# Cross-attention keys prepared inside the query head, first score row begun in its last steps, 3 MB of weights loaded at its end

## The reference

```
x = x + xattn(layernorm(x), ctx)
x = x + attn(layernorm(x))          # 16 heads of 32, with rotation
x = x + ffn(layernorm(x))           # 1408 hidden, ternary weights, int8-like activations
xattn(h, c), 16 heads of 128:
  q     = h @ Wq.T                       # per head 256 x 128
  q_big = rope(q @ w_kc_q[head])         # 256 x 384
  q_r   = q_big @ W_qr[head]             # 256 x 64
  kv_r  = rope(c)                        # 4096 x 128, shared by the heads
  k_r   = kv_r @ W_kr[head]
  attn  = softmax(q_r @ k_r.T)           # 256 x 4096
  ctx   = (attn @ kv_r) @ w_kc_kv[head].T
  out   = concat(ctx) @ Wo.T
```

## Time and profile before

| | |
|---|---|
| median of 3 runs | 612.31 us (609.09 to 613.04) |
| the profiled execution's own time | 611.09 us |
| its span, mean granted TensorE clock | 609.0 us, 0.975 |
| TensorE busy | 543.2 us (89%) |
| DVE busy | 501.3 us (82%) |
| ACT busy | 378.8 us (62%) |
| POOL busy | 169.1 us (28%) |
| DMA moved | 107.40 MB |

### The profile page before, as it was taken

One profiled execution on the slowest core, in us unless ns is written; L12 is line 12 of the kernel. 1 busy time (PEld: TensorE's weight loads), 2 busy tenths in 40 slices (PEclk: granted clock), 3 DMA queues, 4 the chain that ended last, 5 costly groups with the idle time before them and its releaser, 6 DMA issues.

```text
span 609.0 us, 9985 instructions
## 1 busy us (share of the span) xinstructions
PE 543.2 (89%) x3759; PEld 359.7 (59%) x3762; DVE 501.3 (82%) x769; ACT 378.8 (62%) x487; POOL 169.1 (28%) x146
## 2 busy tenths in 40 slices
PE   6989938799989989999999999999979997788896
PEld 3767613266666657666666666666767853355543
DVE  4698858998988888898899998999966656799786
ACT  3154445877767776876767868778785348553332
POOL 0599853001222212212212120210000243455001
PEclk9999988799999999999999999999999999889999
DMA  8976403999999999999999999999997973000000
GB/s 344 328 240 211 129 10 53 168 201 200 209 203 214 200 192 208 208 212 214 204 214 211 210 216 210 211 212 210 206 184 138 396 301 149 0 0 1 2 1 34
DMA packets 287806, 107.40 MB, mean 176 GB/s; under 512 B 276896, under 2 KB 277920, under 8 KB 286368
## 3 DMA queue, kind: packets, MB, share of 16 engines
q1 hardware_dynamic: 287776, 107.01, 80.8%
HBM read 37.26 MB, written 0.52 MB: 62 GB/s over the span
## 4 chain that ended last, share of the span: by engine, by line
PE 47%; DVE 22%; DMA 11%; SPq 8%; issue 5%; POOL 4%; ACT 3%; DVEq 0%; ACTq 0%
DMA pT<-split 10%; PE ps L651 10%; SPq L444 6%; DVE split L1246 6%; PE ps L653 5%; DVE rows L1264 5%; PE ps L633 4%; PE ps L635 4%; PE ps L634 4%; PE ps L755 3%; POOL qrope L484 2%; PE ps L793 2%; DVE anb L1414 2%; PE ps L819 2%; PE ps L698 1%
## 5 line engine op out<-in xcount | busy, mean ns | idle before, releaser
L651 PE MATMUL ps<-pT,VH 128*128 128x256 f16 x1024 | 196.2, 273 | 14.8 <-DMA pT<-split 14.7
L1264 DVE TENSOR_SCALAR_CACHE_REDUCE rows<-ps,qback 128x1024 f32<-128x1024 f32 x128 | 163.6, 1281 | 30.5 <-PE ps L635 30.0
L653 PE MATMUL ps<-pT,VL 128*128 128x128 f16 x1024 | 182.7, 219 | 0.0
L1015 ACT ACTIVATE split<-rows,rz 128x2048 f16<-128x2048 f32 x64 | 124.8, 1994 | 80.6 <-DVE rz L1215 78.2
L1246 DVE SCALAR_TENSOR_TENSOR split<-rows,rz,split 128x2048 f16<-128x2048 f32 x64 | 150.2, 2349 | 1.3 <-ACT split L1015 0.8
L651 PEld LDWEIGHTS ps<-pT,VH 128*128 128x128 f16 x1024 | 100.2, 98 | 64.8 <-DMA pT<-split 28.9
L1001 ACT ACTIVATE rows<-rows,negm 128x2048 f32<-128x2048 f32 x64 | 127.3, 1990 | 10.3 <-DVE negm L1269 10.3
L516 POOL TENSOR_TENSOR ctx_c<-acc 128x128 f32<-128x128 f32 x32 | 36.8, 1151 | 301.1 <-ACT acc L990 301.1
L653 PEld LDWEIGHTS ps<-pT,VL 128*128 128x128 f16 x1024 | 100.4, 98 | 23.4
L633 PE MATMUL ps<-KH,qcur 128*128 128x512 f16 x256 | 98.8, 386 | 9.4 <-DVE qcur L1319 4.6
L634 PE MATMUL ps<-KL,qcur 128*128 128x512 f16 x256 | 98.7, 385 | 0.0
(11 more groups left out here) (182 smaller groups left out, 774.5 us busy)
## 6 DMA issues: line engine op xcount, KB each, us to landing
w_sb<-w SPq DMA_DIRECT2D x3, 2816.0 KB, 16.4
wq_sb<-wq SPq DMA_DIRECT2D x4, 1024.0 KB, 9.9
wo_sb<-wo SPq DMA_DIRECT2D x16, 256.0 KB, 3.5
wkcq_sb<-wkcq SPq DMA_DIRECT2D x4, 768.0 KB, 6.3
keys<-ctxT SPq DMA_DIRECT2D x8, 256.0 KB, 3.4
stage<-ctxT SPq DMA_DIRECT2D x16, 128.0 KB, 4.1
stage<-kcos SPq DMA_DIRECT2D x8, 256.0 KB, 4.0
stage<-ksin SPq DMA_DIRECT2D x8, 256.0 KB, 5.0
```

The lines of the kernel that those rows point to most:

```text
L651: nc.tensor.matmul(bank(6 + r % 2, 0, 256), VH[:, 4 * b + k, :], p.rearrange("p x q -> p (x q)"), start=(b == 0 and k == 0), stop=False)
L653: last = nc.tensor.matmul(bank(6 + r % 2, 0, 128), VL[:, 4 * b + k, :], p[:, 0, :], start=False, stop=(b == 7 and k == 3))
L1015: nc.scalar.activation(split[:, split_slot(r, half), :, 0, :], rows[:, k, half * 2048:(half + 1) * 2048].rearrange("p (b k) -> p b k", k=1 ...
L1264: nc.vector.tensor_scalar(rows[:, k, c * 1024:(c + 1) * 1024], ps[:, score_bank(s) * 512:(score_bank(s) + 2) * 512], qback[:, r // 2:r // ...
```

## The change

- The keys' steps come from a list, `KEY_STEP = (0, 3, 5, 7, 8, 9, 10, 12)`: POOL turns chunk n in step KEY_STEP[n] (now always behind its query sum), DVE adds one step later, ACT sums two steps later.
- The loads of the head are put in a new order, with chunk 0 right after the first `wq` group, and `wq` group 3 behind chunk 5.
- Scale, KH and KL come inside the loop: `key_scale` in step 14, KH in steps 15 to 17, KL in 16 to 18. `qrot` moves to another place in memory, since VH now is written early.
- TensorE does attention steps 32 to 35 in head step 18, 36 and 37 in step 19, 38 and 39 in step 20. DVE's copies of the first row follow its loop.
- SP transposes keys into values two chunks at a time as they are split. Then it loads the first eight parts of `wo` (2 MB) and all of `wkv` (1 MB). In the loop remain the other eight parts of `wo`, as 16 halves of 128 KB behind rows 2 to 17.

The core of the diff:

```
@@ -39,6 +39,8 @@
     SPLIT_STEPS = (12, 14, 16, 17, 18, 19, 20, 21, 22, 23)
     PRODUCT_STEPS = (18, 19, 20, 21, 22, 23)
     EARLY = NCH
+    KEY_STEP = (0, 3, 5, 7, 8, 9, 10, 12)
+    SPLIT_FIRST = (0, 3, 6, NCH)
     STEPS = XH + 6
     QKV_BANK = ((4, 2, 3), (5, 6, 3))
     HPARTS = ((0, 6 * 128), (6 * 128, FF))
@@ -402,33 +404,42 @@
 
             sp.dma_start(x_sb[:, :, :], x_in.rearrange("(t p) d -> p t d", p=128)).then_inc(x_loaded, 16)
             load_wq(0)
+            load_ctx(0)
             load_wkcq(0)
             sp.dma_start(qcos_sb[:, :], qcos).then_inc(qtab_in, 16)
             sp.dma_start(qsin_sb[:, :], qsin).then_inc(qtab_in, 16)
+            load_ctx(1)
             load_wq(1)
             load_wqr(0)
-            load_ctx(0)
             sp.dma_start(wkr_sb[0:RR], wkr[:, 0::2]).then_inc(wkr_in, 16)
             sp.dma_start(wkr_sb[RR:], wkr[:, 1::2]).then_inc(wkr_in, 16)
+            load_ctx(2)
+            load_wq(2)
             load_wkcq(1)
-            load_ctx(1)
-            load_wq(2)
+            load_ctx(3)
+            load_ctx(4)
             load_wkcq(2)
-            load_ctx(2)
+            load_ctx(5)
+            load_wq(3)
+            load_ctx(6)
+            load_ctx(7)
             load_wqr(1)
-            load_wq(3)
-            load_ctx(3)
             load_wkcq(3)
-            for n in range(4, NCH):
-                load_ctx(n)
-            sp.wait_ge(qr_done, XH)
-            sp.wait_ge(kl_done, NCH)
+            sp.wait_ge(qhk_done, XH // 2)
             for k in range(4):
                 key = slice(k * 1024, (k + 1) * 1024)
+                sp.wait_ge(kh_done, 2 * k + 2)
                 sp.dma_start_transpose(VH[:, 8 * k:8 * k + 8, :], KH[:, key]).then_inc(v_in, 16)
+                sp.wait_ge(kl_done, 2 * k + 2)
                 sp.dma_start_transpose(VL[:, 8 * k:8 * k + 8, :], KL[:, key]).then_inc(v_in, 16)
+            sp.wait_ge(qbig_done, XH)
+            for h in range(XH // 2):
+                sp.dma_start(wo_part(wo_sb, h), wo[:, h, :]).then_inc(wo_in[h // 4], 16)
             sp.wait_ge(qabs_done, XH // 2)
-            sp.wait_ge(qbig_done, XH)
+            for k in range(4):
+                heads = slice(k * XH // 4, (k + 1) * XH // 4)
+                sp.dma_start(wkv_sb[:, heads, :], wkv[:, heads, :]).then_inc(wkv_in, 16)
+            sp.wait_ge(qpart_done, XH)
             sp.dma_start(lnp[:, 0], ln_w).then_inc(lnp_in, 16)
             sp.dma_start(lnp[:, 1], ln_b).then_inc(lnp_in, 16)
             sp.dma_start(acs[:, :, 0], acos).then_inc(lnp_in, 16)
@@ -446,11 +457,9 @@
 
             for r in range(2 * XH):
                 turn_row(r)
-                if 1 <= r <= XH:
-                    sp.dma_start(wo_part(wo_sb, r - 1), wo[:, r - 1, :]).then_inc(wo_in[(r - 1) // 4], 16)
-                if XH + 2 <= r < XH + 6:
-                    heads = slice((r - XH - 2) * XH // 4, (r - XH - 1) * XH // 4)
-                    sp.dma_start(wkv_sb[:, heads, :], wkv[:, heads, :]).then_inc(wkv_in, 16)
+                if 2 <= r < XH + 2:
+                    h, cols = XH // 2 + (r - 2) // 2, slice(r % 2 * DM // 2, (r % 2 + 1) * DM // 2)
+                    sp.dma_start(wo_part(wo_sb, h)[:, cols], wo[:, h, cols]).then_inc(wo_in[h // 4], 16)
             sp.wait_ge(av_done, 16 * XH)
             sp.dma_start(wink_sb[:, :, :], w_k).then_inc(win_in, 16)
             sp.dma_start(winq_sb[:, :, :], w_q).then_inc(win_in, 16)
@@ -485,17 +494,14 @@
                                             ALU.add).then_inc(qrope_done, 1)
 
             for p in range(STEPS):
-                if p == 3:
-                    query_sum(p - 2)
-                if p % 2 == 1 and 0 <= (p - 3) // 2 < NCH:
-                    n = (p - 3) // 2
+                query_sum(p - 2)
+                if p in KEY_STEP:
+                    n = KEY_STEP.index(p)
                     s = stage[:, n % 2]
                     pool.wait_ge(ctx_in[n % 2], 80 * (n // 2 + 1))
                     key = keys[:, n * 512:(n + 1) * 512]
                     nc.gpsimd.tensor_tensor(key, key, s[:, 1], ALU.mult).then_inc(kmul_done, 1)
                     nc.gpsimd.tensor_tensor(s[:, 0], s[:, 0], s[:, 2], ALU.mult).then_inc(kmul_done, 1)
-                if p != 3:
-                    query_sum(p - 2)
 
             def head_queries(h):
 
@@ -722,11 +728,13 @@
                         last = nc.tensor.matmul(absorbed(a), wkr_sb[part, n // 2, :], qrT[part, n // 2 % 2, :],
                                                 start=True, stop=True)
                     last.then_inc(qabs_done, 1)
-            query_total(0)
-            for s in range(TURN - 16, TURN - 16 + EARLY):
-                if s == TURN - 16 + EARLY - 2:
-                    query_total(1)
-                attention_step(0, s)
+                if p == 16:
+                    query_total(0)
+                if p >= 18:
+                    first = TURN - 16 + (0, 4, 6, 8)[p - 18]
+                    for s in range(first, TURN - 16 + (4, 6, 8, 8)[p - 18]):
+                        attention_step(0, s)
+            query_total(1)
 
             attention_loop(pe, attention_step, EARLY, AVLAG)
             for t in range(TT):
...
@@ -948,27 +962,21 @@
-                if p % 2 == 0 and 0 <= (p - 4) // 2 < NCH:
-                    n = (p - 4) // 2
+                if p - 2 in KEY_STEP:
+                    n = KEY_STEP.index(p - 2)
-
-            def key_high(n):
-
-                act.wait_ge(kscale_done, 1)
-                key = slice(n * 512, (n + 1) * 512)
-                nc.scalar.activation(KH[:, key], keys[:, key], ACT.Identity, scale=kscale[:, 0:1]).then_inc(kh_done, 1)
-
-            key_high(0)
-            key_high(1)
-            act.wait_ge(qhk_done, XH // 2)
-            act.wait_ge(qfac_done, 1)
-            nc.scalar.activation(qcur[:, 2, 0], QF[:, 0, :], ACT.Identity, scale=qfac[:, 0:1]).then_inc(qcur_first, 1)
-            for n in range(2, NCH):
-                key_high(n)
+                if 15 <= p < 18:
+                    for n in range(SPLIT_FIRST[p - 15], SPLIT_FIRST[p - 14]):
+                        key_high(n)
+                if p == 18:
+                    act.wait_ge(qhk_done, XH // 2)
+                    act.wait_ge(qfac_done, 1)
+                    nc.scalar.activation(qcur[:, 2, 0], QF[:, 0, :], ACT.Identity, scale=qfac[:, 0:1]).then_inc(qcur_first, 1)
+
...
@@ -1296,39 +1311,31 @@
-                if p % 2 == 0 and 0 <= (p - 4) // 2 < NCH:
-                    n = (p - 4) // 2
+                if p - 1 in KEY_STEP:
+                    n = KEY_STEP.index(p - 1)
-
-            def key_low(n):
-
-                key = slice(n * 512, (n + 1) * 512)
-                dve.wait_ge(kh_done, n + 1)
-                nc.vector.scalar_tensor_tensor(out=KL[:, key], in0=keys[:, key], scalar=kscale[:, 0:1], in1=KH[:, key],
-                                               op0=ALU.mult, op1=ALU.subtract).then_inc(kl_done, 1)
-
-            key_scale()
-            query_part(0)
-            key_low(0)
-            query_factor(0)
-            link(nc.vector.tensor_copy(qback[:, 2:3], qunscale[:, 0:1]))
-            key_low(1)
-            dve.wait_ge(qcur_first, 1)
-            nc.vector.scalar_tensor_tensor(out=qcur[:, 2, 1], in0=QF[:, 0, :], scalar=qfac[:, 0:1], in1=qcur[:, 2, 0],
-                                           op0=ALU.mult, op1=ALU.subtract).then_inc(qcur_first, 2)
-            key_low(2)
-            key_low(3)
+                if p == 14:
+                    key_scale()
+                if p == 15:
+                    query_part(0)
+                if p == 17:
+                    query_factor(0)
+                    link(nc.vector.tensor_copy(qback[:, 2:3], qunscale[:, 0:1]))
+                if 16 <= p < 19:
+                    for n in range(SPLIT_FIRST[p - 16], SPLIT_FIRST[p - 15]):
+                        key_low(n)
+                if p == 18:
+                    dve.wait_ge(qcur_first, 1)
+                    nc.vector.scalar_tensor_tensor(out=qcur[:, 2, 1], in0=QF[:, 0, :], scalar=qfac[:, 0:1], in1=qcur[:, 2, 0],
+                                                   op0=ALU.mult, op1=ALU.subtract).then_inc(qcur_first, 2)
+
             attention_step(0, 33)
-            query_part(1)
-            key_low(4)
-            key_low(5)
             attention_step(0, 35)
-            key_low(6)
-            key_low(7)
             attention_step(0, 37)
             attention_step(0, 39)
+            query_part(1)
             attention_loop(dve, attention_step, EARLY, AVLAG)
```

More of the change, by code:

```diff
@@ L64, in program @@
         stage = at("stage", A + 36 * KB, [128, 2, 3, 512])
-        qrot = at("qrot", A + 48 * KB, [128, 2, QC * TOK])
+        qrot = at("qrot", EF + 7 * KB, [128, 2, QC * TOK])
         hT_lo = at("hT_lo", A + 60 * KB, [128, DK, TOK], f32r)
@@ L930, in _, with key_high @@
                     .then_inc(hT_hi_done, 1)
+            def key_high(n):
+                act.wait_ge(kscale_done, 1)
```

(9 more changed lines are left out.)

## The result

The changed kernel takes 623.01 us in the median of 4 runs (622.72 to 625.65), the kernel before, run beside it, 612.67 us (609.09 to 614.97 in 4 runs). The ratio is 1.0184, 95% interval 1.0142 to 1.0225. The forecast was 602, with a range from 594 to 612.

A forecast was written before the change was run, and what follows sets the result against it. It saw a chain of waits led by TensorE, with DMA and the SP queue holding 19%, not arithmetic alone. Head 2.7 late, -2.0 key transposes, -11.0 loop: -10.3 us, median 612.31 to 602, range 594 to 612.

The forecast's parts named there:

- Middle of the head: Head, from the fourth rotation's end at 35.3: addition priced at 0.69 us, chunk 2 added at 41.1, chunk 3 at 49.5.
- Start of the head: Head's first rotations: first starts at 22.1 for 19.36, 2.7 us late; POOL gives back 2.5, fourth ends 0.6 late at 35.3.
- The new wait: Head, wq group 3 queued on SP behind chunk 5: weights there at 57.5, wanted at 47.44; TensorE stands 7.5 us.
- Last steps: Head's end, DVE's remaining work from 59.8: first score at 95.0, maximum at 105.9 against 103.23, 2.7 us late.
- Loads in the loop: Cross-attention loop: four wkv loads gone save 2.6 us, 16 wo halves at half price 8.4; 11.0 saved, bounds 2.6 and 19.1.
- Key transposes: SP before the first row: transposes begin two chunks at a time and finish before that row, saving 2.0 us.
- Loads at the end of the head: SP, wo and wkv loads ahead of the first row's transposes: costed at nothing, up to 3 us if cover went.
- A: Rival, head: no wait for wq group 3, its load landing while POOL is slower; 598, or 590 with halves nearly free; 15%.
- B: Rival, loop: half loads cost like whole ones, the price being the interruption and not the bytes; 610 us; 20%.
- C: Rival: loads at the head's end hold the first transposes, so all rows slip by up to 5 us; 607 us; 8%.
- D: Rival, head: TensorE's granted clock falls after the new stall and stays down; 618, or 627 if halves cost like wholes; 12%.

## Why the prediction was wrong

The mechanisms it named were there, the sizes in the head were not, and one mechanism was missing: VectorE waiting out GpSimd's instruction. The head came 21.2 us late for a forecast of 2.7, 18.5 too much: 10.2 until the fourth `wq` group was there, 7.5 in the last steps, 0.8 from the first score to the maximum. The waits on GpSimd's sums are 1.6 and 3.3 of the 10.2 and the largest part of the 7.5; the load's own time is 3.9 of the 10.2.

*Middle of the head*: the step that failed first. It priced the addition at 0.69 us, from the earlier trace rows, where it began 0.04 us ahead of GpSimd's sum (46.09 and 46.13), and the sum took the wait (2.35). In the changed order the end of the chunk releases both the addition and the next query sum, GpSimd begins first, and the addition waits the sum out: 2.32. Chunk 2 was added by 45.65, not 41.1, chunk 3 by 55.83, not 49.5. Of those 6.3 us, 2.6 came from *Start of the head* (below) and 3.3 from these two additions; GpSimd's sums that began beside VectorE's weight split took 2.85 for the 2.3 of the forecast. The kernel without the sums shows it: 0.69 or 0.70 everywhere. The earlier trace rows did not show the slow form; other additions of the old trace did (2.32 us at 29.88, 2.27 at 82.05).

*Start of the head*: the first rotation began at 22.62, near the 22.1 forecast. But the 2.5 us that GpSimd was to give back did not come: the fourth rotation ended at 37.9, not 35.3, with the addition at 33.14 taking 2.32 behind a wait of 1.74 for GpSimd. Without the sums it ended at 34.73. With the weights first, 3.4 us return as well.

*The new wait*: the mechanism was as foreseen, with its queue and the engines behind it, but both its ends were late. The chunk's issue took 2.63 us (2.7 forecast), but it started at 55.86; and the load took 9.2 us to release ScalarE, not "a little over 5". A chunk of 1 MB was in flight ahead of it and another was issued right behind it, and from 60 to 66 us the DMA engines were busy all the time, at 332 GB/s. That they delayed each other is my reading; no run has the load alone there. The earlier trace rows is of a load in an empty queue; the page of the old kernel had the nearer figure, 9.9 us as the median of its four `wq` loads. TensorE stood 12.14 us, not 7.5. The weights came 10.2 us later than forecast. Taking the wait away gave only 5.6 of it back, as `wqr` was next.

*Last steps*: forecast from 59.8 to 95.0 for the first score, in fact from 70.03 to 112.69, 7.5 us longer. Two slow additions (3.2), eight `KL` in 7.8 us for 5.4, `qtotal` and `qfac` with 1.87 and 1.48 for 0.2 each (2.9) are 8.5; they overshoot by 1.0, and some of the `KL` ran beside GpSimd's `qscaled`, not a sum. From score to maximum it was 11.7, forecast 10.9.

*Loads in the loop*: right in kind, too large. A row with a half took (333.48 - 165.61) / 15 = 11.19 us, so a half costs 0.73 over the 10.46 of the earlier trace rows, 0.71 of a whole; I had taken 0.5, and no row stood behind that: the earlier trace rows holds only loads of 256 KB. The estimate of 0.65 from the Trainium skill (DMA: Bandwidth & Descriptors, Measured) in the prediction was nearer. 16 x 0.30 + 2.6 = 7.4 us, of which the loop shows 5.7, and 6.0 and 4.2 in the two other pairs of kernels. What takes the other 1.7 I can't name. 5.3 us of the forecast gain weren't there.

*Key transposes* (2.0) and *Loads at the end of the head* (nothing) came as written, by the places in the trace: the first row was issued at 134.28, 0.03 behind its low half, and moving the loads out left it at 134.21.

The sum with measured sizes: 21.2 in place of 2.7 for the head, -2.0, and -5.7 - 1.8 for loop and tail in place of -11.0, so +11.7, against the +12.0 of the spans (0.3 lie between maximum and split). The 1.8 are the spread behind the loop, no gain of the change.

*Rivals.* A is out, the wait was there. B is half right: a half costs 0.71 of a whole by the rows. Eight wholes gave the same time as sixteen halves, so the number of interruptions alone doesn't decide; what part of the price is fixed stays open. C is out. D is nearly out: the clock was at 0.5 after the stall, but at 1.00 from 74 us on. The slow stretch cost TensorE 2.4 us (1.22 for 0.70, 2.93 for 1.46, 1.90 for 1.52). The slower side came true, but by VectorE's waits on GpSimd and a load that took longer than I priced it, and neither was a rival of mine; that D's side of the forecast was hit is luck.

## What to carry to other kernels

A duration from the trace holds for its neighbourhood: ask of each instruction that a change moves which other engine's work will start at the same signal, and which of the two starts first, above all of VectorE and GpSimd on SBUF. Take the longer form if the new order lets the other one start first: here 0.1 us decided who waited 1.6. Before a producer is moved ahead of a load in one queue, price that load with what is in flight around it, and ask what is late next once it is gone. Here the part that paid (bytes moved out of a crowded loop into a queue's idle time) was worth 5.1 us alone by the medians (ratio 0.9874), while the rearrangement bundled with it cost 19.0 alone (631.6 against 612.61).

## What the runs showed of the hardware that I had not expected

- VectorE beside GpSimd: an instruction with 128x2 elements took 1.87 us for 0.23, an addition 2.32 for 0.69, always until GpSimd's instruction had ended. It works the other way too: GpSimd's sum took 2.35 us beside an addition that began 0.05 us ahead of it, and 2.85 beside a weight split of 1.23 that did so, for some 1.8 undisturbed.
- The 1 MB load of `wq` took 9.2 us with two chunks of keys around it, against 4.8 in an empty queue; the median of four is 10.1 in the changed kernel and 9.9 in the kernel before.
- A plain load between DMA transposes costs a row time although its data is needed only much later: 0.73 to 0.82 us for 128 KB and 0.64 to 1.31 us for 256 KB. Eight of 256 KB cost as much in all as sixteen of 128 KB.
